# One kernel of window attention and an FP4 feed-forward: attend steps in pairs, four row tiles turned on TensorE, two banks for the last output products

## What is computed

```python
def _L0_attn_ref(x, w_qkv, w_out, b_out):
    qkv = x @ w_qkv
    starts = jnp.arange(0, L - KS + 1, ST)              # KS = 4, ST = 2
    idx = starts[:, None] + jnp.arange(KS)[None, :]
    q, k, v = jnp.split(qkv[:, idx], 3, axis=-1)
    ...
    dots = jnp.einsum('bnqhd,bnkhd->bnhqk', q, k) * scale
    o = jnp.einsum('bnhqk,bnkhd->bnqhd', jax.nn.softmax(dots, axis=-1), v)
    y = o.reshape(B, N, KS, C) @ w_out + b_out
    return zeros.at[:, idx.reshape(-1), :].add(y.reshape(B, N * KS, C))

def _L0_ffn_ref(x, w_gate, w_up, w_down):
    ...
    h = jax.nn.silu(fp4_linear(x, w_gate)) * fp4_linear(x, w_up)
    return fp4_linear(h, w_down)

xn = _layernorm(x, axis=-1)
x = x + _L0_attn_ref(xn, ...) + _L0_ffn_ref(xn, ...)
```

## Time and profile before

| | us |
|---|---|
| median of 3 runs (2204.01 to 2210.74) | 2207.1 |
| the profiled execution's own time | 2204.8 |
| its span, first to last instruction | 2202.7 |
| PE busy | 2148.9 (98% of the span) |
| DVE, POOL, ACT busy | 1663.7, 1219.0, 656.9 |

### The profile page before, as it was taken

One profiled execution on the slowest core, in us unless ns is written; L12 is line 12 of the kernel. 1 busy time (PEld: TensorE's weight loads), 2 busy tenths in 40 slices (PEclk: granted clock), 3 DMA queues, 4 the chain that ended last, 5 costly groups with the idle time before them and its releaser, 6 DMA issues.

```text
span 2202.7 us, 46918 instructions
## 1 busy us (share of the span) xinstructions
PE 2148.9 (98%) x16712; PEld 1037.8 (47%) x16712; DVE 1663.7 (76%) x3108; ACT 656.9 (30%) x1009; POOL 1219.0 (55%) x877
## 2 busy tenths in 40 slices
PE   4999999999999989999999999999999999999999
PEld 1544444544444444444444444444444444444444
DVE  7877877787787666877878778787787777878774
ACT  2342433333343322222222222222222232222221
POOL 3256767666665554555555555555555555555553
PEclk9999999999999999999999999999999999999999
DMA  9656656575766544333333333433334333343333
GB/s 267 189 122 175 157 142 175 133 191 133 177 149 167 136 166 111 82 87 83 78 90 80 87 83 78 94 75 87 86 80 91 77 83 89 77 92 74 87 74 68
DMA packets 449418, 251.82 MB, mean 114 GB/s; under 512 B 367282, under 2 KB 373938, under 8 KB 449300
## 3 DMA queue, kind: packets, MB, share of 16 engines
q1 hardware_dynamic: 448404, 246.99, 46.1%
q10 hardware_dynamic: 576, 2.10, 0.2%
q0 software_dynamic: 320, 0.97, 0.2%
HBM read 99.01 MB, written 59.77 MB: 72 GB/s over the span
## 4 chain that ended last, share of the span: by engine, by line
PE 75%; POOL 10%; issue 9%; DVE 2%; DMA 1%; SPq 0%; ACT 0%; POOLq 0%; DVEq 0%; ACTq 0%
PE acc L978 10%; PE prj L1350 7%; PE ops L1350 7%; PE acc L1331 5%; PE acc L1335 5%; PE acc L1332 5%; PE prj L978 3%; PE ops L1352 3%; PE prj L1352 3%; PE sps L1333 2%; PE acc L1334 2%; PE sps L1336 2%; PE acc L1336 2%; PE sps L1334 2%; PE acc L1333 2%
## 5 line engine op out<-in xcount | busy, mean ns | idle before, releaser
L978 PE MATMUL acc<-late 128*128 128x512 f16 x2304 | 516.8, 380 | 11.0 <-DMA late<-xh 10.9
L978 PEld LDWEIGHTS acc<-late 128*128 128x128 f16 x2304 | 218.4, 98 | 270.7 <-issue 16.5
L209 POOL TENSOR_TENSOR qk<-qk,xh 128x1408 f32<-128x1408 f32 x64 | 165.6, 2588 | 230.1 <-DVE qk L246 230.1
L1225 DVE SCALAR_TENSOR_TENSOR qk<-acc,row_gains,xh 128x512 f32<-128x512 f32 x64 | 48.0, 751 | 260.2 <-ACT xh L1290 260.2
L204 POOL TENSOR_TENSOR qk<-qk,xh 128x1024 f32<-128x1024 f32 (+1 forms) x128 | 177.3, 1386 | 111.2 <-DVE xh L225 111.2
L214 POOL TENSOR_TENSOR v<-qk,v 128x1408 f16<-128x1408 f32 x64 | 183.0, 2859 | 100.3 <-ACT v L256 100.3
L1350 PE MATMUL prj<-late,qk 128*128 128x512 f16 x704 | 214.6, 379 | 0.7 <-DMA qk<-v 0.7
L1350 PE MATMUL ops<-late,qk 128*128 128x512 f16 x704 | 214.6, 379 | 0.0
L256 ACT ACTIVATE v<-qk 128x1408 f16<-128x1408 f32 x64 | 88.1, 1377 | 367.3 <-POOL qk L209 367.3
L1331 PE MATMUL acc<-late,turned 128*128 128x512 f16 x512 | 194.0, 379 | 0.4 <-DVE qk L1225 0.4
L1335 PE MATMUL acc<-late,turned 128*128 128x512 f16 x512 | 194.1, 379 | 0.0
(11 more groups left out here) (158 smaller groups left out, 4440.0 us busy)
## 6 DMA issues: line engine op xcount, KB each, us to landing
normed<-late SPq DMA_DIRECT2D x64, 256.0 KB, 3.0
res<-in_L_attn_x SPq DMA_DIRECT2D x64, 256.0 KB, 2.9
attended<-res SPq DMA_DIRECT2D x64, 256.0 KB, 2.5
raw<-normed SPq DMA_DIRECT2D x64, 256.0 KB, 2.7
v<-attended SPq DMA_DIRECT2D x64, 256.0 KB, 2.7
out<-v SPq DMA_DIRECT2D x64, 256.0 KB, 2.0
late<-in_L_attn_x SPq DMA_DIRECT2D x62, 256.0 KB, 3.8
ready<-turned SPq DMA_DIRECT2D x36, 256.0 KB
```

The source lines that it names most:

```text
L209: pool.tensor_tensor(blocks(v), blocks(v), spread(s[3]), ALU.mult).then_inc(q["valued"], 1)
L978: last = pe.matmul(out, lhsT, rhs, start=(at == 0), stop=(at == n - 1))
```

## The change

1. **Attend in pairs.** `PAIRS = [(0, 1), (0, 1), (2, 3), (2, 3), (4, 4), (5, 6), (5, 6), (7, 8), (7, 8)]`. The second step of a pair writes the other half of the `ops` banks and no longer waits for `o_out`; ACT copies both out when the second is done. The order strings put the two next to each other on PE.
2. **Four row tiles turned on PE.** The first four tiles of batch 0 are turned by 8 transposes each (`turn_first_rows`, T) into the banks `sps` and `ops`, and copied out by ACT (`rows_turned`, y). SP's four DMA transposes of them go.
3. **Two banks for the last output products.** In the last batch odd `p` steps write `acc[2]`, and `project_out(i)` waits for `final(i - 2)`.
4. **New orders** of all five engines' strings, score steps put next to each other among them.
5. `spread_weights` and `turn_weights` for `a = 0` wait for the last step of the batch before, not for the last but one; `first_rounder` waits for a rounding step; `F1` waits for `final` too.

```diff
+PAIRS = [(0, 1), (0, 1), (2, 3), (2, 3), (4, 4), (5, 6), (5, 6), (7, 8), (7, 8)]
...
+    flip = [bank.bitcast(F16).rearrange("p (a k t) -> p a k t", a=2, k=KC)
+            for bank in (sps[:, 0, :], sps[:, 1, :], ops[:, 0, :], ops[:, 1, :])]
+    def out_bank(b, i):
+        return acc[2] if isinstance(b, int) and b == B - 1 and i % 2 else prj
...
+        def rows_turned(b, i):
+            act.wait_ge(flipped, i + 1)
+            act.activation(xt[:, :, :, i * P:(i + 1) * P], flip[i], ACT.Copy).then_inc(xt_in[i], 16)
...
         def attended(b, a):
-            act.wait_ge(pv_done, at(b, ATT, a))
-            src = ops[:, :, 0:2 * P].rearrange("p g (c q) -> p c g q", c=KC)
+            act.wait_ge(pv_done, at(b, ATT, PAIRS[a][1]))
+            src = ops[:, :, (a - PAIRS[a][0]) * 2 * P:(a - PAIRS[a][0] + 1) * 2 * P].rearrange("p g (c q) -> p c g q", c=KC)
...
+        def turn_first_rows(b, i):
+            pe.wait_ge(c_in, 32)
+            pe.wait_ge(xlo_done, at(b, TPB, i))
+            for a in range(2):
+                for k in range(KC):
+                    last = pe.transpose(flip[i][:, a, k, :], xh[:, i, a, k * P:(k + 1) * P], eye[:, :])
+            last.then_inc(flipped, 1)
...
         def attend(b, a):
+            half = (a - PAIRS[a][0]) * 2 * P
...
-            pe.wait_ge(o_out, at(b, ATT, a - 1))
+            if a == PAIRS[a][0]:
+                pe.wait_ge(o_out, at(b, ATT, a - 1))
...
         def project_out(b, i):
             pe.wait_ge(o_lo, at(b, TPB, i))
-            pe.wait_ge(final, at(b, TPB, i - 1))
-            three_products(prj[:, :], ...
+            if isinstance(b, int) and b == B - 1:
+                pe.wait_ge(final, at(b, TPB, max(i - 2, -1)))
+                if i == 1:
+                    pe.wait_ge(qkv_out, at(b, QKV, QKV - 1))
+            else:
+                pe.wait_ge(final, at(b, TPB, i - 1))
+            three_products(out_bank(b, i)[:, :], ...
...
-                "p6' s5 v4 s4 a0 v5 a1 s6 p7' s7 v6 s8 v7 a2 q0+ q1+ q2+ a3 q3+ q4+ q5+ a4 q6+ q7+",
+                "v4 p6' s5 s4 v5 v6 a0 a1 s6 p7' s7 s8 v7 q0+ q1+ q2+ a2 a3 q3+ q4+ q5+",
-                "v0+ p0 s0+ a5 v1+ s1+ p1 s2+ a6 v2+ p2 a7 v3+ q8+ q9+ q10+ q11+ p3 q12+ q13+ p4 a8 q14+ s3+ p5 q15+",
+                "q6+ a4 q7+ v0+ v1+ p0 v2+ s0+ s1+ s2+ p1 v3+ s3+ a5 a6 p2 q8+ p3 a7 a8 q9+ q10+ p4 q11+ q12+ q13+ "
+                "q14+ q15+ p5",
```

More of the change, by code:

```diff
@@ L317, in attention @@
     acc, prj, sps, ops = shared.acc, shared.prj, shared.sps, shared.ops
+    flip = [bank.bitcast(F16).rearrange("p (a k t) -> p a k t", a=2, k=KC)
+            for bank in (sps[:, 0, :], sps[:, 1, :], ops[:, 0, :], ops[:, 1, :])]
+    flipped = sem("flipped")
+    def out_bank(b, i):
+        return acc[2] if isinstance(b, int) and b == B - 1 and i % 2 else prj
     w_in, o_in, c_in, b_in = [sem(f"w_in{k}") for k in range(KC)], sem("o_in"), sem("c_in"), sem("b_in")
@@ L563, in spread_weights @@
             pool.wait_ge(p_done, at(b, NG, a // GT))
-            pool.wait_ge(p_turned, at(b, ATT, a - 2))
+            pool.wait_ge(p_turned, at(b, ATT, a - 2 if a else -1))
             pool.tensor_tensor(pw[:, a % 2].rearrange("p h b (g s) -> p h (b g) s", s=SLOTS),
@@ L754, in turn_weights @@
             dve.wait_ge(p_spread, at(b, ATT, a))
-            dve.wait_ge(pv_done, at(b, ATT, a - 2))
+            dve.wait_ge(pv_done, at(b, ATT, a - 2 if a else -1))
             dve.transpose(pt[:, a % 2].rearrange("p h q -> p (h q)"),
@@ L779, in finish @@
             dve.wait_ge(biased, at(b, TPB, i))
-            dve.scalar_tensor_tensor(res[:, i % 4, :], prj[:, :], sc[:, 5:6], res[:, i % 4, :],
+            dve.scalar_tensor_tensor(res[:, i % 4, :], out_bank(b, i)[:, :], sc[:, 5:6], res[:, i % 4, :],
                                      ALU.mult, ALU.add).then_inc(final, 1)
@@ L947, in first_rounder @@
         def first_rounder(b, k):
+            if k == 1:
+                act.wait_ge(rows.q["rounded"], 1)
             rounder(act, rows.q, rows.raw[:, k, :], rows.rounder, k)
@@ L955, in scalar @@
         batches(act,
[8 rows of a table removed]
-                {"x": high_rows, "q": qk_out, "v": v_out, "e": exponential, "o": attended, "h": out_high,
[8 rows of a table added]
+                {"x": high_rows, "y": rows_turned, "q": qk_out, "v": v_out, "e": exponential, "o": attended, "h": out_high,
                  "B": unit_rounder, "H": high_unit, "W": weights_high, "U": out_weights_high,
@@ L1042, in attend @@
                     r = slice(2 * BLK * g, 2 * BLK * (g + 1))
-                    last = pe.matmul(ops[DH * (h % 2):DH * (h % 2) + DH, g, h // 2 * DH:(h // 2 + 1) * DH],
+                    last = pe.matmul(ops[DH * (h % 2):DH * (h % 2) + DH, g,
+                                         half + h // 2 * DH:half + (h // 2 + 1) * DH],
                                      vals[r, h * DH:(h + 1) * DH], pt[r, a % 2, h % 2 * (HEADS // 2) + h // 2, :],
@@ L1049, in project_out @@
             pe.wait_ge(o_lo, at(b, TPB, i))
-            pe.wait_ge(final, at(b, TPB, i - 1))
-            three_products(prj[:, :], [((oh[:, i % 4, 0, k], oh[:, i % 4, 1, k]),
+            if isinstance(b, int) and b == B - 1:
[4 more added lines that the diff above has]
+                pe.wait_ge(final, at(b, TPB, i - 1))
+            three_products(out_bank(b, i)[:, :], [((oh[:, i % 4, 0, k], oh[:, i % 4, 1, k]),
                                                (wo[:, 0, k], wo[:, 1, k])) for k in range(KC)]).then_inc(proj_done, 1)
@@ L1076, in tensor @@
         batches(pe,
[6 rows of a table removed]
-                {"q": project_qk, "v": project_v, "s": scores, "a": attend, "p": project_out, "M": column_tops, "W": out_ready,
[7 rows of a table added]
+                {"q": project_qk, "v": project_v, "s": scores, "a": attend, "p": project_out, "T": turn_first_rows,
+                 "M": column_tops, "W": out_ready,
                  "F": first_products})
@@ L1123, in feed_forward @@
     dps = [shared.ops[:, 1, :], shared.prj[:, :]]
-    acc_free = [ended.copied, ended.copied + ended.masked, ended.masked + ended.evacuated]
+    acc_free = [ended.copied, ended.copied + ended.masked + ended.projected, ended.masked + ended.evacuated]
     def await_all(engine, ends):
```

## The result

The changed kernel took 2253.3 us (median; 2251.1 to 2255.6) where the one before took 2205.95 on the same chip: ratio 1.021, 95% interval 1.019 to 1.0233. The forecast was 2180.5, in a range of 2171 to 2195, with 0.03 for slower. The case that came true is the last rival, slower. Its chain is in the trace, but at one of four places only, and its chance was far too small.

What follows compares the result with a forecast made beforehand. PE, 98% busy, was taken as the bound. Seams 15.6, start 7.5 and tail 3.5 us, with 0 for new orders, made 26.6 us off, from 2207.1 to 2180.5 us, range 2171 to 2195.

Steps and rivals of the forecast that it cites:

- the last rival, slower: At `a6`, DVE's rounding step waits for ACT and POOL; 3.8 us a turn cancels the gain, 5 gives 2215; chance 0.03.
- What bounds the kernel: Whole kernel: PE, busy 2148.9 of 2202.7 us, so only what it does or waits for counts.
- Seams: Changes between kinds of step on PE: their cost falls from 34.3 to 18.7 us, 15.6 us won.
- The rival that seams stay: Steps of the same kind side by side on PE keep their seams: 8.6 us back, 2189.1; chance 0.12.
- Start: PE's first large product: at 25.6 us instead of 33.12, 7.5 us won by turning four tiles on PE.
- that rival: At the start, turning is slow or the last weight part late: 2 us won instead of 7.5, 2186; chance 0.10.
- the prediction's own sign of being wrong: Batch 0: the prediction is wrong if PE idles between the fourth and the sixteenth q step.
- Two banks at the end: Last batch's output products: waits for the `finish` just before, 0.93 us each, go; 3.5 us won, between 1 and 6.
- New orders, "0, the waits of a turn left at 2.1 us": Turn of the loop: waits stay at 2.1 us, change 0, between 1 us less and 1.5 us more per turn.
- near places: In the loop, besides `a6`: `a3` and the EDGE score step behind `pack_edges`, with 0.5 to 1 us of room each.

Runs made afterwards that it cites:

- e6_pairs: The kernel before with attend steps in pairs in all batches but the last, helpers' orders changed only as pairs need: 2207.4 us, ratio 1.0011.
- e9_scores: e5_ends with score steps put next to each other on PE alone, no helper's order touched: 2204.8 us, ratio 0.9996 to the kernel before.
- e5_ends: The kernel before with four tiles turned on PE and two banks at the end, otherwise its old orders: 2198.8 us, ratio 0.9977.
- e8_late_w6: The kernel before with only the masking of the next scores moved ahead of the weight turns on DVE: 2229.5 us, ratio 1.0112.

## Why the prediction was wrong, step by step

- **What bounds the kernel:** right. PE's timeline decided everything, and DVE (74% busy) was never the bound by its busy time.
- **Seams:** the mechanism was right and the attend pairs have the size: 370.83 to 371.94 is 1.11 us, two steps of 0.48 and one seam of 0.15. Three score steps (`s0+ s1+ s2+`, 347.70 to 349.82) take 2.12 where 3 x 0.57 + 0.12 = 1.83 was forecast. The rival that seams stay fell for attend pairs. That a seam saved is time won failed: `e6_pairs` gave nothing and `e9_scores` less than nothing.
- **Start:** 8.2 us for 7.5, by the chain given; the first q step at 24.91 for 25.6. The transposes are fast: eight took 1.01 us, 126 ns each in a row, so that rival fell. The Trainium skill (TensorE: Matmul & The Clock Gate, Part 4: PE-mode transpose) has about 275 ns for one inside a kernel; for eight in a row the measurement decides. But the gain is not kept whole: in `e5_ends` the first q step is 6.8 us earlier and the first feed-forward product only 6.3, of which 2.0 come from the tail. PE's first score step, behind nine large steps in both kernels, shows where it goes: 58.20 before, 53.87 in `e5_ends`, 4.3 earlier. Three q steps in, PE waits 2.00 us there for ACT's copy of q (the prediction's own sign of being wrong, one step early), and more products run at the slow pace. The changed kernel has no such wait: its first score step stands behind ten large steps, at 53.84, so nine were done 6.9 us earlier than before. Part of the 8.2 is the luck of one execution: with the same start as before, `e6_pairs` and `e8_late_w6` began at 31.64 and 31.10, not at 33.12.
- **Two banks at the end:** forecast 3.5, measured 2.0 in `e5_ends` (last EDGE score step to first F: 47.8 us for 49.8). The row read for it, is the seventh product, `p6`, and the seven waits for `finish` were 0.31 to 1.42 us, not 0.93 each time. The waits for `finish` went from `p4` on; a wait of 2.0 for `attended` and one of 1.8 for a low part came in their place. Mechanism right, term too large.
- **New orders, "0, the waits of a turn left at 2.1 us":** this is the step that failed. The waits at the four places are 8.4 us a turn (50.2 in six), and the profile's idle time in the attention grew by 44.0 us in all. At `a6` the sum was 6.95 us of DVE work against 6.6 us of PE's; measured were 9.39 (349.91 to 359.30) against 6.76. The difference is 1.56 us of waiting for ACT, 0.46 more in L821 and 0.46 more in L760 than their means in the earlier trace rows, while POOL was at work. The prediction named the wait for ACT and set it aside "by the means". POOL's spread of the weights, due at about 358.15, was in no term: even at the forecast's 6.95 DVE would have stood waiting for it. The other three places it did not find: `f4'` behind four `normalize` steps that wait for loads of x through POOL's roots (`p5`, 3.44); `o3` behind a rounding step on ACT (`a4`, 1.4); the copy of `q6+` behind `h0` (`v1+`, 1.4). They were waits of PE in nearly every turn, and the search for near places had looked only at weights and scores.
- **A cost that stood nowhere:** the clock, 23.2 us. The prediction noted that the start runs at half speed and did not ask what a wait of 3 us in the loop does. The longest wait of these kinds in the loop before was 1.1 us, so the trace of before could not show it there. The nearest sign was the slow start, behind a wait of 10.43, though the granted clock is given as full in it.
- **Slower:** the point from which the gain is gone was put at 3.8 us at `a6` in each turn. Measured are 2.9 at `a6`, 3.2 at `p5`, and 1.2 to 2.2 at `a4` and 1.4 at `v1+` in most turns, 8.4 in sum, with the clock on top. A rival that adds one place only was too narrow, and 0.03 had no ground: the new orders moved steps on all five engines, and one move can cost 25 us (`e8_late_w6`).

## What to carry to other kernels

In a kernel whose order is written by hand on five engines and whose bound engine is 98% busy, an order is worth more than the seams that it saves: price each step that moves ahead of something the bound engine waits for with its slowest instance and its own waits, not with its mean. Make a structural change first on the old orders, measure it there, and move one step at a time. Where the bound engine's clock can fall, a new wait of 3 us can cost twice its length, as at `a6` here (2.95 and 2.8 us). And read every input of the step that waits: at `a6` two chains, on DVE and on POOL, ended within 0.5 us of each other.

## What the hardware showed that was not expected

- The granted clock fell behind ten of the fifteen waits of 2.0 us or more that PE has in the changed kernel from 50 to 800 us. Behind five it did not, though they are of like length (2.15 to 3.30 us): the attend step below took 0.69 us, the one at 359.53, behind 2.95, took 1.13. What makes the difference was not tried.

```profile
254.54 0.69 PE L1074 MATMUL ops<-pt,v 64*64 64x64 f32 x32 [2.91 <-DVE pt L767]
```

- After `a6` at the lower level, one attend step (1.07 for 0.63) and one output product (4.96 for 2.59) lost 2.8 us, almost as much as the wait of 2.95 ahead of them.
- Runs of score products, 64 in each step at 9 ns apiece, can stall for lack of anything the profile names: 0.5 us for a pair in `e9_scores`, 0.28 for a run of three in the changed kernel, and there once 2.00 us in the middle of a step (below), with the clock low behind it. That it is the supply of instructions is a guess.

```profile
60.48 0.49 PE L1052 MATMUL sps<-qk 64*32 64x32 f32 x35 [2.00 <-issue]
```
